# A drain of GpSimd in every turn of the routed loop, and the last scatter indices taken earlier

## The reference, cut to what matters

```
scores = jax.nn.sigmoid(x @ gate_w.T) + bias
topk_w, topk_idx = jax.lax.top_k(scores, TOPK)
topk_w = topk_w / (jnp.sum(topk_w, axis=-1, keepdims=True) + 1e-20)
...
g = jnp.einsum('th,eih->eti', x, Wg)
u = jnp.einsum('th,eih->eti', x, Wu)
z = jax.nn.silu(g) * u
zw = z * cw.T[:, :, None]
out = jnp.einsum('eti,ehi->th', zw, Wd)
out = out + jax.nn.silu(x @ Sg.T) * (x @ Su.T) @ Sd.T
```

## Time and profile before

| | us |
|---|---|
| median of 3 executions | 683.39 |
| lowest, highest | 683.23, 683.39 |
| the profiled execution, its own time | 683.01 |
| the profiled execution, span of the trace | 681.2 |
| PE busy in the span | 666.1 |
| POOL busy in the span | 175.1 |

### The profile page before, as it was taken

How to read it: one execution, slowest core, us unless ns; L and a number is a source line. 1 busy time by engine, 2 the same in 40 slices (tenths; PEclk the granted TensorE clock), 3 DMA queues, 4 the chain that set the end, 5 groups by cost and what they waited for, 6 DMA issues and landing times.

```text
span 681.2 us, 9804 instructions
## 1 busy us (share of the span) xinstructions
PE 666.1 (98%) x2424; PEld 397.8 (58%) x2425; DVE 335.6 (49%) x867; ACT 219.3 (32%) x626; POOL 175.1 (26%) x226
## 2 busy tenths in 40 slices
PE   9999999999999999999999999999999999999993
PEld 7565444466777766777776777674444444444441
DVE  3995224534334556586766777455333333333331
ACT  4575522212344433545445463220111111111110
POOL 2365100001000000005414143355123332333334
PEclk9999999999999999999999999999999999999998
DMA  9999999331400200001103015314776757769545
GB/s 338 407 421 419 422 421 427 109 109 56 161 1 0 94 1 0 1 1 62 63 2 154 8 57 188 121 70 123 255 196 139 154 92 189 184 138 242 95 76 62
DMA packets 60403, 103.18 MB, mean 151 GB/s; under 512 B 7200, under 2 KB 32544, under 8 KB 59712
## 3 DMA queue, kind: packets, MB, share of 16 engines
q1 hardware_dynamic: 30320, 73.48, 28.9%
q0 software_dynamic: 8816, 18.00, 13.3%
q10 hardware_dynamic: 21232, 11.28, 5.7%
HBM read 46.60 MB, written 56.26 MB: 151 GB/s over the span
## 4 chain that ended last, share of the span: by engine, by line
PE 91%; DMA 2%; another core or an unknown queue 2%; issue 1%; ACT 1%; ACTq 1%; DVE 1%; POOL 0%; POOLq 0%; DVEq 0%
PE ps L1275 55%; PE ps L1470 12%; PE ps L1261 4%; PE ps L1439 4%; PE ps L1455 4%; PE ps L1386 3%; PE ps L1396 3%; PE ps L1387 3%; DMA out<-rq,sidx 1%; PE ps L1408 1%; PE ps L1322 1%; PE ps L1242 1%; PE ps L1291 1%; DMA rq<-slot_rows 1%
## 5 line engine op out<-in xcount | busy, mean ns | idle before, releaser
L1275 PE MATMUL ps<-kv,rq 128*128 x432 | 192.8, 594 | 2.1 <-DVE rq L969 1.6
L1275 PE MATMUL ps<-zT,r 128*128 128x256 f32 (+1 forms) x552 | 132.5, 395 | 0.1
L1275 PEld LDWEIGHTS ps<-kv,rq 128*128 128x128 f32 x432 | 78.8, 190 | 89.5 <-issue 89.2
L1275 PEld LDWEIGHTS ps<-zT,r 128*128 128x128 f32 x552 | 103.5, 190 | 23.5 <-issue 10.1
L1470 PE MATMUL ps<-r 128*128 128x512 f32 x192 | 85.3, 593 | 0.0
L656 POOL DMA_INDIRECT out<-rq,sidx x36 | 56.6, 1573 | 108.8 <-DMA out<-rq,sidx 76.5
L581 POOL TENSOR_SCALAR ve<-mv 128x1 f32<-128x1 f32 x32 | 7.1, 223 | 262.1 <-DVE mv L988 262.1
L787 ACT ACTIVATE r<-ps,snm 128x128 f32<-128x128 f32 x128 | 45.2, 365 | 58.6 <-DVE snm L1104 57.5
L1200 DVE TENSOR_TENSOR rq<-ps,rq 128x256 f32<-128x256 f32 x36 | 15.3, 424 | 95.7 <-ACT rq L839 90.2
L1470 PEld LDWEIGHTS ps<-r 128*128 128x128 f32 x192 | 35.1, 190 | 37.8 <-issue 37.8
L839 ACT ACTIVATE rq<-ps 128x256 f32<-128x256 f32 x36 | 13.8, 383 | 119.5 <-PE ps L1275 119.5
(11 more groups left out here) (181 smaller groups left out, 866.2 us busy)
## 6 DMA issues: line engine op xcount, KB each, us to landing
slot_rows<-rq SPq DMA_DIRECT2D x4, 8192.0 KB, 50.1
kv<-in_experts SPq DMA_DIRECT2D x54, 256.0 KB
rq<-slot_rows ACTq DMA_DIRECT2D x138, 64.0 KB
r<-in_Wq SPq DMA_DIRECT2D x1, 3072.0 KB, 19.8
r<-in_Wo SPq DMA_DIRECT2D x2, 1536.0 KB, 6.3
r<-in_ctx SPq DMA_DIRECT2D x8, 256.0 KB, 9.1
xr<-in_x SPq DMA_DIRECT2D x8, 256.0 KB, 9.5
second_norm_rows<-zrow SPq DMA_DIRECT2D x8, 256.0 KB, 2.1
```

The costliest lines, as they stand in the source:

```text
L1275: mm = pe.matmul(out, lhs(k), rhs(k), start=(k == 0), stop=(k == n - 1))
```

## The change

Two things are changed, both on GpSimd. In every turn of the loop a `pool.drain()` is executed for the odd tile, behind its index copy and ahead of the waits for the other parity's scatter and for the rows. And the index copies of tiles `tail`+2 and `tail`+3 are executed in tile `tail`, behind that tile's own index copy, with a semaphore of their own, `s_sl2`; the last two tiles then wait for `s_sl2` and not for `s_si`. On the way the read of `tab` that gives the column has moved into the helper `scatter_index`, so that it stands behind the wait for the scatter of tile i-2 and not ahead of it.

```diff
+        s_sl2 = sem("last_scatter_indices_ready")
...
-            def add_rows(i, par, before, last=False):
+            def scatter_index(i, column, done):
 
                 col = pool.value_load(tab[0:1, bass.ds(i, 1)], min_val=0, max_val=P)
+                pool.tensor_copy(sidx[:, column:column + 1], ids[:, bass.ds(col, 1)]).then_inc(done, 1)
+
+            def add_rows(i, par, before, last=False, ahead=None):
+
                 index = sidx[:, 2 + par:3 + par] if last else sidx[:, par:par + 1]
-                if last:
-                    pool.tensor_copy(index, ids[:, bass.ds(col, 1)]).then_inc(s_si, 1)
                 if not isinstance(i, int) or i >= 2:
                     pool.wait_ge(s_ys[par], i * 8 if par == 0 else i * 8 - 8)
                 if not last:
-                    pool.tensor_copy(index, ids[:, bass.ds(col, 1)]).then_inc(s_si, 1)
+                    scatter_index(i, par, s_si)
+                if ahead is not None:
+                    ahead()
 
                 if before is not None:
                     pool.wait_ge(s_ys[1 - par], before)
-                pool.wait_ge(s_si, i + 1)
+                if last:
+                    pool.wait_ge(s_sl2, 2)
+                else:
+                    pool.wait_ge(s_si, i + 1)
                 pool.wait_ge(s_yc, i + 1)
...
             with pool.Fori(4, tail, 2) as n:
-                for i, par in ((n, 0), (n + 1, 1)):
-                    add_rows(i, par, rows_before(i))
+                add_rows(n, 0, rows_before(n))
+                add_rows(n + 1, 1, rows_before(n + 1), ahead=pool.drain)
+
+            def last_indices():
+
+                for i in (2, 3):
+                    scatter_index(tail + i, i, s_sl2)
+
             for i in range(4):
-                add_rows(tail + i, i % 2, rows_before(tail + i), i >= 2)
+                add_rows(tail + i, i % 2, rows_before(tail + i), i >= 2, last_indices if i == 0 else None)
```

## The result

The changed kernel takes 692.45 us (median of four executions, 690.46 to 693.65) against 683.39 (683.23 to 683.88). The ratio is 1.0135, with a 95% interval of 1.0119 to 1.0151: 9.1 us slower. The profiled execution of it is the fastest of the four, 690.46, so that its trace shows 7.5 us of the loss.

The account below looks back on a forecast made before the run. PE paces the routed loop; GpSimd's scatter times and 3 us last drain gate the end. 683.01 - 2.44 = 680.57, plus 0.38 for the runs' median, gives 680.95, say 681.0; range 680.4 to 686.5.

Parts of the forecast that it names:

- The 14 drains in the loop: GpSimd, odd tiles of the loop: each drain covers two scatters and takes 0.33 us (the first 0.57), at cost 0.
- What a drain costs: GpSimd's drains: price grows with the number of software DMAs since the last drain, 0.079 to 0.106 us each.
- 2.5 us of cover: Tile 31 on GpSimd: drain ends near 655.1, while its scatter waits for the row copy until 657.60 anyway.
- rival 4: Loop drains wait for scatters in flight, plus a fixed 2.6 to 3.0 us behind the landing: about 720 us; chance 0.08.
- rival 3: Loop drains wait until scatters in flight have landed, then are cheap: +1 to +11 us, taken as 690; chance 0.09.
- The last drain: GpSimd's drain at the program's end: five scatters left to cover, 0.57 us instead of 3.009, a gain of 2.44.
- The index copies and the moved read: GpSimd, copies ahead in tile 32 and later read of `tab`: cost 0 (read at most 0.1), gain 0 to 0.1 us.
- PE stays full: Routed loop: PE remains busy from 486 to 655 us, as before, so GpSimd's work there does not reach the end.
- six turns: Assumed number of the loop's 14 turns whose next even tile is an expert's first, each losing 1.1 to 2.7 us.
- The tile 31 estimate: Loop's last turn, if drains wait for landings: tile 31 alone slips by only 0.6 us, so it could still be faster.
- the longest flight: Scatter flights of 6.6 us, which would make turns of 11.9 us last 13.5, against PE's 10.8.

## Why the prediction was wrong

The step that failed is *The 14 drains in the loop*, with the reading of *What a drain costs* under it. I took a drain's price to be a matter of the DMAs' number alone, 0.33 us each, inside 2.5 us of cover. The runs show two parts: the flight of whatever is in the air, and then the clearing. With one scatter nearly always in flight (4.9 us of every 5.4), the first part is the whole flight.

The rows allowed it. The drain of L632 lasted past a landing, and I wrote down that reading and preferred the other on the strength of the 0.174 us of an empty drain. That row speaks against a fixed price behind a landing, rival 4, and not against waiting, rival 3. The law joins all of them: 0.05 + 0.041 x 65 = 2.7 us behind the landing at L632. The prediction had 2.6 there from rounded times; to the hundredth it is 486.44 - 483.73 = 2.71, and 2.71 in every trace that has this drain.

Point by point. The last drain: right, 0.463 us against 0.57 forecast, and the gain of 2.5 is there. The index copies and the moved read: right, nothing either way. PE stays full: wrong, through a buffer that the prediction never priced, the row buffer that DVE may only write when the scatter of tile i-2 has landed. Rival 3, with a chance of 0.09, is what happened, and its 690 lay 2.5 us under the median. Its six turns, an estimate from one row, are the number that the starts of the scatters in the trace of before give, and its loss in them, 6.6 to 16 us less 3 of slack, holds the 9.8 that was measured (6.8 us lost by PE and 3.0 by which the scatters were late at the end). It did not name the row buffer, through which PE was held. The tile 31 estimate, 0.6 us late in the last turn and still faster over all, was for a drain in that turn alone, which no run has.

The prediction also took 6.6 us for the longest flight. That range comes from the landings of 18 odd tiles; the trace of before holds no landing of an even tile. Its timeline shows one all the same, since the index copy of tile 8 waits for the landing of tile 6:

```profile
523.87 1.57 POOL L656 DMA_INDIRECT out<-rq,sidx  x1 [3.53 <-DMA out<-rq,sidx]
...
532.30 0.18 POOL L649 COPY sidx<-ids 128x1 int32 x1 [1.36 <-DMA out<-rq,sidx]
```

The copy starts 8.4 us behind that scatter. The long flights of the changed kernel (8.7, 9.0 and 8.3 us at tiles 6, 14 and 22) were there before the change, in the very turns that lead up to an expert's first tile.

The page "VectorE: DVE Perf Modes" of the Trainium skill, section "The DRAIN you can't avoid", gives its constant 12 ns for the boilerplate drains that the runtime puts around a program. The last drains here belong to the program's own closing barrier, and the figure does not carry over to them as the prediction let it: GpSimd's took 0.382, 0.463, 1.441, 3.009 and 6.161 us in these runs, where SP's took 13 ns.

## What to carry to other kernels

Before an instruction that empties an engine is put into a loop, ask what is in flight there and not only what the engine has left to do: on GpSimd the drains of these runs waited for every scatter that it had in flight. Put it where the next instruction waits for that landing anyway, and rarely; two such drains gave 2.4 us where fourteen in the loop took 9. And a price that can be read in two ways from a single row deserves its own chance: here the long drain ended behind a landing, and that was the better half of the evidence.

## What the runs showed of the hardware

- GpSimd's drain waits for its scatters in flight: 13 of 14 ended 0.13 us behind the landing, after flights of 5.0 to 9.0 us. With nothing in flight it took 0.44 us at the same place, the index copy of 0.18 beside it.
- Its clearing has a price for each DMA since the last drain: 0.082 us with all landed (4, 5, 17 and 36 scatters: 0.382, 0.463, 1.441, 3.009 us), of which about half is hidden when a flight is still to be waited for (2, 5, 10, 22 and 32 scatters: 0.13, 0.25, 0.45, 0.95 and 1.36 us behind the landing; 65 placing and plain DMAs: 2.71). With 101 DMAs it was 6.161, less than that rate gives; why stays open.
